# Linear attention with values and context as the stationary operands, two heads on two column halves of TensorE

## The chip, the core and the metric

The kernel runs on one core of a Trainium2 chip. The metric is the device time of one execution in microseconds (us), the median of several runs.

## The reference

On 1024 nodes of 512 features, a normalised `x` goes through a two-layer graph convolution and, beside it, through two Performer layers (linear attention with kernel features, then a feed-forward network); both results are added to `x`, and a mixture of experts follows. The kernel computes the Performer layers first. The change touches their attention alone. For each of the two layers, with 8 heads of 64 features and 256 random features (`M`), it is:

```python
qp = ratio * (exp(dd_q - diag_q - max_over_features) + 1e-4)     # (heads, nodes, 256)
kp = ratio * (exp(dd_k - diag_k - max_over_all) + 1e-4)          # (heads, nodes, 256)
k_sum = kp.sum(nodes)
d_inv = 1.0 / einsum('nm,m->n', qp, k_sum)
ctx   = einsum('nm,nd->md', kp, v)                               # (heads, 256, 64)
attn  = einsum('nm,md,n->nd', qp, ctx, d_inv)
x = x + (attn @ Wo + bo)
```

where `dd` are the projections of the queries and keys on the random features.

## The kernel before

All products run on TensorE; a large f32 product is written as three f32r products of high and low parts (L528 to L530), while the attention's own products are plain f32. PSUM is two rings of four banks of 128 x 512: ring A (`psA`), emptied mostly by ScalarE, and ring V (`psV`), emptied by VectorE. The order of use of every ring is written out by hand: `A_JOBS` and `MIX_V` number the jobs, TensorE waits until the job four places earlier has been emptied, and each emptying engine counts the jobs it has taken. The four engines' programs follow the same generator, `attention_order` (L127), so that the order of the work is one list.

The heads go in four pairs. A step `g` (16 in a layer, four to a pair) handles two node tiles of 128 for both heads of a pair. In a step:

- `ddq`: scores of the queries against the projection (`scores`, L627), one head on the upper and one on the lower 64 rows of the array, into two banks of ring A. VectorE takes the maximum over features (L1626) and forms the bias (L1629); ScalarE exponentiates into `work[:, 0:2]` (L1063).
- `ddk`: the same for the keys of the next pair, four tile pairs, two in each of a pair's first two steps; VectorE copies them out with a running maximum (L1532). GpSimd then takes the maximum over partitions (`kall`, L1317), VectorE forms `kbias` (`k_bias`, L1541), and ScalarE exponentiates the keys in place (`exp_k`, L1020).
- `tr`: eight transposes of the previous step's query exponentials (L712), so that features lie on partitions. ScalarE copies them back (`take_turned`, L1044), adding the constant 1e-4; `work[:, 2:4]` has one buffer, so this waits for the attention product before.
- `at`: the attention product of step g - 2 (L734 to L740): for each head, two node tiles and two halves of the features, the turned queries (128 x 128) stand in the array and 65 columns of the context move past: 64 values and the key sum. VectorE takes the reciprocal of the sum's column, 128 x 2 (L1634), and multiplies into `V` (L1636).
- `ctx`: in each pair's third step (L717 to L729): for each head and each half of the features, the key exponentials (128 x 128) stand and 130 columns of `V` move past: both heads' values, with a column of ones on each side, which gives the key sums. The constant 1e-4 enters as one more matmul with `vsum`, the values summed over tiles. VectorE copies the head's own 65 columns out (L1621).

After the last step the outputs, which have nodes on partitions, are turned by 32 transposes (L743 to L746, jobs `("o", h, k)` of ring A); ScalarE copies the high parts (L1078) and VectorE subtracts the low parts (L1646) into `hT`, and the output projection `wo` reads them (L748).

The queues: SP loads the weights, GpSimd splits them and reduces the key maxima in one queue of its own. In it a weight's split (`load(3, ...)`, waiting for the last query projection) lies between the key maxima of pairs 0 and 1.

## Time and profile before

| what | us |
|---|---|
| median of 3 runs (lowest, highest) | 1158.26 (1157.27, 1162.53) |
| the profiled execution's own time | 1157.11 |
| its span in the trace | 1155.3 |
| mean granted TensorE clock | 0.981 |

The profile is of one execution. A row of a group has the instruction's line in the kernel, engine, operation, the tiles written and read, shapes, count, busy time and mean duration. In the timeline a row merges instructions of the same kind that follow each other: its first start, the time from that to the end of its last, and their count. Matmuls overlap, so what one costs is the distance from its start to the next one's.

### The profile page before, as it was taken

The numbers are of one execution on the slowest core, as the hardware profiler recorded it, in microseconds if no ns is written. First come the engines' busy times: TensorE is split into PE (matmuls) and PEld (weight loads), VectorE is DVE, ScalarE is ACT, GpSimd is POOL, SyncE is SP. The second block draws the span as 40 slices with busy tenths as digits, with TensorE's granted clock in tenths as the row PEclk, the third lists the DMA queues.
The fourth block names the chain that finished last, engine by engine and source line by source line (L and its number), as shares of the span: only waits on it lengthen the run. The fifth ranks groups of instructions, "written<-read, shape, count | busy, mean of one in ns | idle before, by whom it ended". The sixth has DMA issues, their size and how long they took to land.

```text
span 1155.3 us, 16126 instructions
## 1 busy us (share of the span) xinstructions
PE 1083.4 (94%) x5992; PEld 881.8 (76%) x5992; DVE 707.9 (61%) x1530; ACT 366.2 (32%) x671; POOL 149.1 (13%) x141
## 2 busy tenths in 40 slices
PE   3999799999999999999898999999999999999986
PEld 2777699888777777776898977777778888777653
DVE  7576777479676567457665479764653117723667
ACT  4234466525321211136566325221300011001132
POOL 4230202000000000300202000000000705000036
PEclk8999999999999999999999999999999999999897
DMA  6230101002312112000101004211337201100001
GB/s 210 84 117 1 38 2 38 1 5 92 90 48 64 56 47 78 1 1 1 38 1 38 1 5 130 72 46 55 108 148 246 74 1 37 35 1 1 1 18 55
DMA packets 34654, 60.16 MB, mean 52 GB/s; under 512 B 19440, under 2 KB 20400, under 8 KB 33936
## 3 DMA queue, kind: packets, MB, share of 16 engines
q1 hardware_dynamic: 12688, 41.21, 10.9%
q10 hardware_dynamic: 21888, 17.87, 4.8%
q8 instruction: 53, 0.87, 0.3%
q14 instruction: 25, 0.20, 0.1%
HBM read 48.59 MB, written 10.49 MB: 51 GB/s over the span
## 4 chain that ended last, share of the span: by engine, by line
PE 79%; DVE 11%; ACT 4%; issue 4%; POOL 1%; DMA 0%; ACTq 0%; POOLq 0%; DVEq 0%
PE ps_a L528 10%; PE ps_a L530 10%; PE ps_a L529 10%; PE ps_v L528 10%; PE ps_v L529 9%; PE ps_v L530 9%; PE ps_a L885 5%; PE ps_v L725 4%; PE ps_v L736 3%; PE ps_a L549 2%; PE ps_a L660 2%; DVE expk L1532 2%; ACT work L1063 1%; DVE qmax L1626 1%; PE ps_v L614 1%
## 5 line engine op out<-in xcount | busy, mean ns | idle before, releaser
L528 PE MATMUL ps_a<-ht_hi,w_hi 128*128 128x512 f32 x488 | 193.8, 397 | 2.7 <-DVE w_lo L1798 0.9
L530 PE MATMUL ps_a<-ht_hi,w_lo 128*128 128x512 f32 x488 | 191.6, 393 | 0.0
L529 PE MATMUL ps_a<-ht_lo,w_hi 128*128 128x512 f32 x488 | 191.3, 392 | 0.0
L974 ACT ACTIVATE work<-ps_a,col_sb 128x512 f32<-128x512 f32 x96 | 66.7, 719 | 203.0 <-PE ps_a L530 144.7
L528 PEld LDWEIGHTS ps_a<-ht_hi,w_hi 128*128 128x128 f32 x488 | 92.5, 189 | 26.0 <-DVE headmask_r L1497 1.3
L1651 DVE TENSOR_TENSOR xm<-ps_v,xm 128x512 f32<-128x512 f32 x80 | 55.2, 690 | 86.0 <-PE ps_v L530 85.5
L530 PEld LDWEIGHTS ps_a<-ht_hi,w_lo 128*128 128x128 f32 x488 | 92.3, 189 | 19.9
L529 PEld LDWEIGHTS ps_a<-ht_lo,w_hi 128*128 128x128 f32 x488 | 92.4, 189 | 19.4
L528 PE MATMUL ps_v<-w_hi,f_hi 128*128 128x512 f32 x256 | 101.7, 397 | 0.0
L528 PE MATMUL ps_v<-w_hi,ht_hi 128*128 128x512 f32 x224 | 92.0, 411 | 9.7 <-issue 5.8
L530 PE MATMUL ps_v<-w_hi,f_lo 128*128 128x512 f32 x256 | 99.7, 389 | 0.0
L529 PE MATMUL ps_v<-w_lo,f_hi 128*128 128x512 f32 x256 | 99.6, 389 | 0.0
L529 PE MATMUL ps_v<-w_lo,ht_hi 128*128 128x512 f32 x224 | 89.8, 401 | 0.0
L530 PE MATMUL ps_v<-w_hi,ht_lo 128*128 128x512 f32 x224 | 89.5, 399 | 0.0
L1422 DVE CAST ht_hi<-work 128x512 fp32r<-128x512 f32 x56 | 33.1, 590 | 78.6 <-PE ps_a L530 65.2
L1063 ACT ACTIVATE work<-ps_a,qbias 128x256 f32<-128x256 f32 x128 | 50.5, 476 | 86.6 <-PE ps_a L549 71.1
L974 ACT ACTIVATE work<-ps_a,gcol_sb 128x512 f32<-128x512 f32 x24 | 16.5, 689 | 176.8 <-PE ps_a L530 171.8
L725 PE MATMUL ps_v<-v_sb,expk 128*128 128x130 f32 x512 | 63.2, 277 | 0.0
L736 PE MATMUL ps_v<-ctx_sb,work 128*128 128x65 f32 x512 | 61.8, 274 | 1.1 <-DVE ctx_sb L1621 0.6
L736 PEld LDWEIGHTS ps_v<-ctx_sb,work 128*128 128x128 f32 x512 | 59.6, 192 | 3.3 <-DVE expk L1532 1.6
L725 PEld LDWEIGHTS ps_v<-v_sb,expk 128*128 128x128 f32 x512 | 59.7, 191 | 1.1
L528 PEld LDWEIGHTS ps_v<-w_hi,ht_hi 128*128 128x128 f32 x224 | 43.5, 194 | 22.0 <-issue 9.5
(238 smaller groups left out, 1964.9 us busy)
## 6 DMA issues: line engine op xcount, KB each, us to landing
stage<-wstream SPq DMA_DIRECT2D x62, 512.0 KB, 3.7
adj_d<-adj_win ACTq DMA_DIRECT2D x16, 256.0 KB, 2.9
adj<-adj_d ACTq DMA_DIRECT2D x2, 2048.0 KB, 12.3
xt_d<-xt_hi SPq DMA_DIRECT2D x2, 1024.0 KB, 5.0
xt_d<-xt_lo SPq DMA_DIRECT2D x1, 2048.0 KB, 11.4
ht_hi<-xt_d ACTq DMA_DIRECT2D x1, 2048.0 KB, 7.7
ht_lo<-xt_d ACTq DMA_DIRECT2D x1, 2048.0 KB, 12.4
x_again<-x ACTq DMA_DIRECT2D x8, 256.0 KB, 9.3
```

What stands on the lines that cost most here:

```text
L528: nc.tensor.matmul(ps, left[0], right[0], start=first, stop=False)
L529: nc.tensor.matmul(ps, left[0], right[1], start=False, stop=False)
L530: return nc.tensor.matmul(ps, left[1], right[0], start=False, stop=last)
L549: last = nc.tensor.transpose(ps[:, nodes(n)], source, ident[:])
L660: nc.tensor.matmul(ps, hot_low[:, c, :], hot_key[:, c, :], start=c == 0, stop=False)
L725: nc.tensor.matmul(context, expk[g % 2][:, j, t, nodes(m)], V[:, t, g, :], start=t == 0, stop=False)
L736: last = nc.tensor.matmul(ps[:, n * (DH + 1):(n + 1) * (DH + 1)], work[:, 2 + j, nodes(2 * m + n)], ctx_sb[:, pair % 2, j, m, :], start=m ...
L885: nc.tensor.matmul(ps, Pr[i][:, t, nodes(m)], adj[:, t, half(h)].bitcast(f32r), start=False, stop=False)
L974: nc.scalar.activation(work[:, n % 4, :], psA[:, i % BANKS, :], func, **how).then_inc(a_empty, 1)
L1063: last = nc.scalar.activation(work[:, j, M * n:M * (n + 1)], psA[:, i % BANKS, M * n:M * (n + 1)], ACT.Exp, scale=DN, bias=qbias[:, g % 4, ...
L1422: nc.vector.tensor_copy(hi, work[:, n % 4, :]).then_inc(high, 1)
L1651: nc.vector.tensor_tensor(Xm[:, t, :], ps, Xm[:, t, :], ALU.add).then_inc(v_empty, 1)
```

## The change

What it does, in the order of the diff:

- The order of the steps is new. The context of a pair is made in two halves of four node tiles: the first at the end of the fourth step of the pair before (for pair 0 at the end of step 0), the second at the end of the pair's second step. Key scores of the next pairs come in a pair's first and third step, those of the third step behind the turns.
- `context`: the values of one head (128 x 64) stand in one column half of the array, those of the other head in the other, and 256 columns of key exponentials move past each. The constant 1e-4 is one full-width matmul ahead of the first half. Key sums come from ones standing in 32 columns: two heads by two tiles on four column quarters.
- VectorE copies the first half into `ctx_t` and adds the second. `turn_context` transposes the two value blocks, and two matmuls against a head mask gather the sums; VectorE copies these to `ctx_sb`, scaling the sums.
- `attend`: the context of each head (128 x 64), and then its key sum repeated over 64 columns, stand in a column half; 256 columns of turned queries move past. Outputs come out with features on partitions, and the sums already repeated over them. One bank holds both heads.
- VectorE's reciprocal is over 128 x 256, its product over 128 x 256.
- The 32 output transposes and their eight jobs are gone. ScalarE copies the high parts from `V` to `hT`, three blocks in each of steps 14 and 15 and two at the end; VectorE subtracts the low parts, three behind each of the attention steps 12 and 13 and two at the end. The output projection waits for 7 of 8 parts for its first four tiles and for all for the others.
- ScalarE exponentiates the keys tile by tile, four activations in each step. `k_bias` of the next pair moves from VectorE's third step to its second.

The diff, cut to its core (on TensorE, then ScalarE, then VectorE):

```diff
 def attention_order():
         if g < STEPS:
             yield "ddq", g
-            if s < 2 and pair + 1 < NH // 2:
-                yield "ddk", g
-        if s == 2 and g < STEPS:
-            yield "ctx", pair
+            if s == 0 and pair + 1 < NH // 2:
+                yield "ddk", (pair + 1, range(0 if g == 0 else 2, 4))
+            if s == 2:
+                yield "turn_ctx", pair
         if 1 <= g <= STEPS:
             yield "tr", g - 1
+        if s == 2 and pair + 2 < NH // 2:
+            yield "ddk", (pair + 2, range(2))
         if g >= 2:
             yield "at", g - 2
+        if g == 0 or s == 3 and pair + 1 < NH // 2:
+            yield "ctx", (0 if g == 0 else pair + 1, 0)
+        if s == 1 and g < STEPS:
+            yield "ctx", (pair, 1)
+
+OUT_PARTS = [(pair, h) for h in range(H) for pair in range(NH // 2 - 1)] + [(NH // 2 - 1, h) for h in range(H)]
...
+                ones = V[:, 0, 0, 0:1]
+
+                def context(pair, part_):
+                    ps = bank("v", ("ctx", pair, part_))
+                    tiles = range(NT // 2 * part_, NT // 2 * (part_ + 1))
+                    pe.wait_ge(expk_done, L * NH * NT + 2 * NT * pair + NT * (part_ + 1))
...
+                    if part_ == 0:
+                        nc.tensor.matmul(ps[:, 0:M], vsum[:, pair, 1:1 + P], eps_k[:].to_broadcast([P, M]), start=True,
+                                         stop=False)
+                    for t in tiles:
+                        for j in range(2):
+                            nc.tensor.matmul(ps[DH * j:DH * (j + 1), 0:M], V[:, t, pair, 1 + DH * j:1 + DH * (j + 1)],
+                                             expk[pair % 2][:, j, t, :], start=part_ == 1 and t == tiles[0],
+                                             stop=t == tiles[-1])
+                    for t in tiles[0::2]:
+                        for j in range(2):
+                            for i in range(2):
+                                n = 2 * j + i
+                                last = nc.tensor.matmul(ps[32 * n:32 * (n + 1), M:2 * M], ones.to_broadcast([P, 32]),
+                                                        expk[pair % 2][:, j, t + i, :], start=t == tiles[0],
+                                                        stop=t == tiles[-2])
...
+                def turn_context(pair):
+                    ps = bank("v", ("turn_ctx", pair))
+                    written_v(("ctx", pair, 1))
+                    for m in range(MT):
+                        nc.tensor.transpose(ps[:, nodes(m)], ctx_t[:, nodes(m)], ident[:])
+                    for m in range(MT):
+                        last = nc.tensor.matmul(ps[:, M + 2 * m:M + 2 * (m + 1)], ctx_t[:, nodes(MT + m)], headmask[:, 0, 0:2],
+                                                start=True, stop=True)
...
+                def attend(g):
+                    pair, s = divmod(g, NT // 2)
+                    ps = bank("v", ("at", g))
+                    if s == 0:
+                        written_v(("turn_ctx", pair))
+                    written_a(("tr", g, 1))
+                    for columns, values in ((slice(0, M), slice(0, DH)), (slice(M, 2 * M), slice(DH, DH + 1))):
+                        for m in range(MT):
+                            for j in range(2):
+                                left = ctx_sb[:, pair % 2, m, j, values]
+                                last = nc.tensor.matmul(ps[DH * j:DH * (j + 1), columns],
+                                                        left.to_broadcast([P, DH]) if columns.start else left,
+                                                        work[:, 2 + j, M * m:M * (m + 1)], start=m == 0, stop=m == MT - 1)
+                                if columns.start and m == MT - 1:
+                                    last.then_inc(at_half if j == 0 else v_full, 1)
...
-                written_v(("at", STEPS - 1, 1))
-                for h in range(H):
-                    for k in range(KT):
-                        turn(bank("a", ("o", h, k)), [V[:, 4 * h + n, k, 1:1 + P] for n in range(4)], a_full)
                 slot = weight_slot("o")
                 for t in range(NT):
-                    written_a(("o", t // 4, KT - 1))
+                    pe.wait_ge(o_split, L * H * KT + (len(OUT_PARTS) if t >= 4 else len(OUT_PARTS) - 1))
...
                         if g:
-                            act.wait_ge(v_full, v0 + (MIX_V[("at", g - 1, j)] + 1))
+                            act.wait_ge(*((v_full, v0 + (MIX_V[("at", g - 1)] + 1)) if j else (at_half, L * STEPS + g)))
...
+                def high_out(pair, h):
+                    act.wait_ge(v_empty, v0 + done(MIX_V[("at", 4 * pair + 2 * h + 1)]))
+                    nc.scalar.activation(hT[0][:, pair, half(h)].rearrange("p (t n) -> p t n", n=P), V[:, 4 * h:4 * h + 4, pair, 1:1 + P],
+                                         ACT.Copy).then_inc(o_high, 1)
...
+                    pair = (g + 3) // 4
+                    if 0 < pair < NH // 2:
+                        part_ = (s + 3) % 4
+                        exp_k(pair, 4 * part_, 4 * (part_ + 1))
+                    if g == STEPS - 2:
+                        act.wait_ge(v_full, v0 + (MIX_V[("ctx", NH // 2 - 1, 1)] + 1))
+                    if g >= STEPS - 2:
+                        for n in range(3 * (g - STEPS + 2), 3 * (g - STEPS + 3)):
+                            high_out(*OUT_PARTS[n])
                 take_turned(STEPS - 1)
...
+                def take_attended(g):
+                    pair, s = divmod(g, NT // 2)
+                    ps = job("at", g)
+                    dve.wait_ge(at_half, L * STEPS + g + 1)
+                    nc.vector.reciprocal(rden[:, g % 2, :], ps[:, M:2 * M]).then_inc(rden_done, 1)
+                    dve.wait_ge(rden_done, L * STEPS + g + 1)
+                    nc.vector.tensor_tensor(V[:, 2 * s:2 * s + 2, pair, 1:1 + P], ps[:, 0:M].rearrange("p (t n) -> p t n", n=P),
+                                            rden[:, g % 2, :].rearrange("p (t n) -> p t n", n=P), ALU.mult).then_inc(v_empty, 1)
...
+                    elif what == "ddq":
+                        bound_queries(g)
+                        if g % 4 == 1 and g // 4 + 1 < NH // 2:
+                            k_bias(g // 4 + 1)
+                    elif what == "ctx":
+                        pair, part_ = g
+                        if L == 0 and part_ == 1 and pair < 3:
+                            (blocks, keys, bounds)[pair]()
+                        take_context(pair, part_)
...
+                    elif what == "at":
+                        if g == STEPS - 1:
+                            low_out(len(OUT_PARTS) - 2)
+                        take_attended(g)
...
+                        if STEPS - 4 <= g < STEPS - 2:
+                            for n in range(3 * (g - STEPS + 4), 3 * (g - STEPS + 5)):
+                                low_out(n)
+                low_out(len(OUT_PARTS) - 1)
```

## Rows read from the trace of the kernel before

**Rows 1.** The page: busy time, share of the span and instructions of each engine.
```profile
PE 1083.4 (94%) x5992; PEld 881.8 (76%) x5992; DVE 707.9 (61%) x1530; ACT 366.2 (32%) x671; POOL 149.1 (13%) x141
```

**Rows 2.** Window: a pair of layer 0. Length; PE, PEld, DVE, ACT, POOL busy; clock; DMA.
```profile
171.73:199.00 27.27, 26.06 (x265) 24.85 (x265) 20.24 (x66) 17.59 (x41) 7.04 (x5) 1.00 0.10 26
```

**Rows 3.** Timeline of TensorE: start, time to the last one's end, instruction, count [idle before].
```profile
130.09 1.95 PE L725 MATMUL ps_v<-v_sb,expk 128*128 128x130 f32 x16
131.87 0.39 PE L727 MATMUL ps_v<-vsum,eps_k 128*128 128x130 f32 x2
...
137.72 1.97 PE L736 MATMUL ps_v<-ctx_sb,work 128*128 128x65 f32 x16 [0.57 <-DVE ctx_sb L1621]
...
218.09 1.90 PE L736 MATMUL ps_v<-ctx_sb,work 128*128 128x65 f32 x16
```

**Rows 4.** Timeline of TensorE: key scores on two row halves, then transposes.
```profile
121.74 0.28 PE L633 MATMUL ps_v<-proj_hi,k_part 64*128 64x256 f32 x2
121.86 0.28 PE L633 MATMUL ps_v<-proj_lo,k_part 64*128 64x256 f32 x2
...
123.04 0.28 PE L633 MATMUL ps_v<-proj_hi,k_part 64*128 64x256 f32 x2
123.25 1.09 PE L549 MATMUL ps_a<-ident,work 128*128 128x128 f32 x8
```

**Rows 5.** Timeline of TensorE: 8 stationary columns (L614) between products with 128.
```profile
100.53 0.39 PE L530 MATMUL ps_a<-ht_hi,w_lo 128*128 128x512 f32 x1
100.76 0.40 PE L614 MATMUL ps_v<-sq_hi,headmask_r 128*8 128x512 f32 x1
...
101.23 0.39 PE L528 MATMUL ps_a<-ht_hi,w_hi 128*128 128x512 f32 x1
```

**Rows 6.** Waits of TensorE: us in total, times, longest.
```profile
PE ps_a L633 <- ACT work L1063: 15.6, 12, 2.8
```

**Rows 7.** Timeline of GpSimd: the key maximum of pair 1, layers 0 and 1.
```profile
135.78 0.37 POOL L1317 PARTITION_ALL_REDUCE kall<-kmax  x1 [7.30 <-issue]
...
562.60 0.37 POOL L1317 PARTITION_ALL_REDUCE kall<-kmax  x1 [7.38 <-issue]
```

**Rows 8.** Groups by line: instructions, busy us, mean ns | idle before, releasers.
```profile
L1063 ACT ACTIVATE work<-ps_a,qbias 128x256 f32<-128x256 f32 x128 | 50.5, 476 | 86.6 <-PE ps_a L549 71.1 <-DVE qbias L1629 14.7
L1626 DVE TENSOR_REDUCE qmax<-ps_a 128x2 f32<-128x512 f32 x64 | 43.7, 684 | 13.3 <-PE ps_a L633 13.3
L1051 ACT ACTIVATE work<-ps_a,eps_k 128x512 f32<-128x512 f32 x64 | 42.9, 701 | 5.1 <-PE ps_v L736 4.7
...
L1636 DVE TENSOR_TENSOR v_sb<-ps_v,rden 128x128 f32<-128x128 f32 x64 | 18.7, 292 | 2.2
...
L1642 DVE TENSOR_TENSOR xm<-xm,rows_sb 128x512 f32<-128x512 f32 x16 | 12.3, 767 | 0.0
...
L1634 DVE RECIPROCAL rden<-ps_v 128x2 f32<-128x2 f32 x64 | 10.7, 167 | 24.5 <-PE ps_v L736 24.2
...
L1078 ACT ACTIVATE ht_hi<-ps_a 128x512 fp32r<-128x512 f32 x16 | 8.9, 600 | 6.2 <-PE ps_a L549 6.2
```

**Rows 9.** Timeline of TensorE at both layers' ends of attention; a window of layer 1.
```profile
228.86 4.52 PE L549 MATMUL ps_a<-ident,v_sb 128*128 128x128 f32 x32 [0.59 <-DVE v_sb L1636]
233.14 0.48 PE L528 MATMUL ps_v<-w_hi,ht_hi 128*128 128x512 f32 x1
...
644.24 1.90 PE L736 MATMUL ps_v<-ctx_sb,work 128*128 128x65 f32 x16
...
655.01 5.67 PE L549 MATMUL ps_a<-ident,v_sb 128*128 128x128 f32 x32 [0.59 <-DVE v_sb L1636]
660.44 0.48 PE L528 MATMUL ps_v<-w_hi,ht_hi 128*128 128x512 f32 x1
...
655.00:657.00 2.00, 1.99 (x10) 1.99 (x11) 0.28 (x1) 0.65 (x2) 0.00 (x0) 0.53 0.00 0
```

**Rows 10.** One line's instructions (L1869): duration ns min/median/max, starts, form.
```profile
L1869 DVE RECIPROCAL gate<-gate x2: 177/178/178, 1071.7 to 1114.4; 128x4 f32<-128x4 f32 x2
```

More of the change, by code:

```diff
@@ L118 @@
     + query_ring()
-    + [("o", h, k) for h in range(H) for k in range(KT)]
     + ffn_ring_a()
@@ L155, in ring_v_attention @@
         if what == "ddk":
-            yield from ddk_jobs(*ddk_ahead(g))
-            if g == 0:
+            yield from ddk_jobs(*g)
+            if g[0] == 1:
                 yield "turned", 3
-        elif what in ("ctx", "at"):
-            yield from ((what, g, j) for j in range(2))
+        elif what == "ctx":
+            yield (what, *g)
+        elif what in ("turn_ctx", "at"):
+            yield what, g
 MIX_V = numbered(
@@ L698, in mix_layer @@
                 sum_squares(len(QK_ORDER) - 1)
+                ones = V[:, 0, 0, 0:1]
[3 more added lines that the diff above has]
+                    pe.wait_ge(expk_done, L * NH * NT + 2 * NT * pair + NT * (part_ + 1))
+                    if pair == 0 and part_ == 0:
+                        pe.wait_ge(vsum_added, L * (NT - 1) + NT)
+                    if part_ == 0:
[13 more added lines that the diff above has]
+                                                        stop=t == tiles[-2])
+                                if t == tiles[-2]:
+                                    last.then_inc(*((v_full, 1) if n == 3 else (ctx_parts, 1)))
@@ L743, in mix_layer @@
[L743 to L746 removed]
+                    elif what == "ctx":
+                        context(*g)
+                    elif what == "turn_ctx":
+                        turn_context(g)
+                    else:
+                        attend(g)
                 slot = weight_slot("o")
@@ new lines, in bound_queries @@
+                def bound_queries(g):
+                    pair, s = divmod(g, NT // 2)
+                    for j in range(2):
+                        i = MIX_A[("ddq", g, j)]
+                        dve.wait_ge(a_full, a0 + (i + 1))
+                        nc.vector.tensor_reduce(qmax[:, g % 2, j, :], psA[:, i % BANKS, :].rearrange("p (t m) -> p t m", m=M),
+                                                axis=AX.X, op=ALU.max).then_inc(qmax_done, 1)
+                        dve.wait_ge(qmax_done, L * 2 * STEPS + (2 * g + j + 1))
+                        nc.vector.scalar_tensor_tensor(out=qbias[:, g % 4, j, :], in0=qmax[:, g % 2, j, :], scalar=-DN,
+                                                       in1=ndiag[:, 0, 2 * s:2 * s + 2, 2 * pair + j], op0=ALU.mult,
+                                                       op1=ALU.add).then_inc(qbias_ready, 1)
@@ L1607, in mix_layer @@
                 for what, g in attention_order():
-                    pair, s = divmod(g, NT // 2)
                     if what == "ddk":
-                        ddk(*ddk_ahead(g))
-                        if g == 0:
+                        ddk(*g)
+                        if g[0] == 1:
                             take_turned(3)
-                        continue
-                    if what == "tr":
-                        continue
-                    if what == "ctx" and L == 0 and g < 3:
-                        (blocks, keys, bounds)[g]()
```

109 lines of the change are left out of this document (36 added, 73 removed).

## The prediction

> **What bounds the kernel now.** I read the page's busy shares first: TensorE is busy 94% of the span, VectorE 61%, ScalarE 32% [rows 1], so time is lost or won on TensorE. Then a stage by windows: one pair of heads in the middle of layer 0's attention takes 27.27 us, with TensorE busy 26.06, VectorE 20.24 and ScalarE 17.59 [rows 2]; each layer has four. So a pair costs what TensorE does in it plus about 1.2 us of waits, and the change must be priced in TensorE's instructions.
>
> Next, the pitch of these instructions (the distance of starts; durations overlap). Every plain f32 matmul is two records, each with its own weight load. In the context product 16 records of 130 columns start within 1.78 us, 0.111 each; in the attention product 16 records of only 65 columns take (1.90 - 0.27) / 15 = 0.108 each [rows 3]. Half the columns at the same pitch: the 65-column records wait for their 128-column weight loads, and at 130 columns the streaming just shows above that. So before: a pair's context is 72 records, 4 x 18 x 0.111 = 8.0 us, and a step's attention 16 x 0.108 = 1.74 us, 6.96 a pair.
>
> **What the records cost after.** Stationary and moving operands change places: 256 columns now move past 64 or 32 stationary ones. No row shows a 256-column f32 record. Below, it cannot beat the f32r scores, whose 256 columns pass once in about 0.12 [rows 4]; above, streaming that grows with the columns gives 0.111 x 256 / 130 = 0.22. I take T = 0.22, because the 130-column record is the nearest row and lies above the weight-load pitch.
>
> Do two column halves run at once? No row shows it; two row halves do: the scores come as pairs (x2), one pair per 0.12 us [rows 4]. I take it that column halves can too; if not, each record costs a full T. But a score is one record, and an f32 matmul is two. Issued in program order, the second record of head 0 waits for the first (same columns), and the first record of head 1 stands behind it. So records overlap in steps: head 0's second with head 1's first, and so on; n matmuls take (n + 1) T. With four quarters nothing more is won in this order: again one matmul per T, not four per 2 T.
>
> **The sum, part by part, for a pair.** Attention: 8 matmuls a step, 9 T = 1.98 us, 7.92 a pair (before 6.96). Context, first half: eps matmul 2 T, eight value matmuls, eight ones matmuls, one T to run out, 19 T; second half 17 T; together 36 T = 7.92 (before 8.0). Turning the context: two transposes and two matmuls against the head mask, 6 records at 0.11 = 0.66. Together 16.5 against 14.96: **+1.54 a pair, +6.2 a layer**. Three of the 16 attention steps lie in the tail, counted apart below: 0.7 of the 6.2 goes there, 5.5 stays.
>
> Changing between tile shapes: from half rows to full rows the scores' last pair starts at 123.04, frees the array at 123.16, and the transposes start at 123.25: 0.09 [rows 4]. From 128 to 8 stationary columns and back, 3 starts in 0.70 us, 0.23 each [rows 5], is the pitch of matmuls that change nothing, so I count column shapes at nothing (at most 0.09 each, some eight a pair, 6 us in all). Key scores moved behind the turns add a trip or two: +0.3 a layer.
>
> Waits in the steps. TensorE waits 15.6 us in all for ScalarE's exponentials, in 12 waits up to 2.8 [rows 6]; two of about 2.8 lie at the layers' starts, which leaves 5.0 a layer. With half a context behind every second step there is always cover for them: they go. In their place comes a smaller one: the attention product is now signalled for both heads almost together, so ScalarE starts to empty the next turned block (2 x 0.70 [rows 8]) only at its end. TensorE has the query scores (6 x 0.12 + 0.09 = 0.8 [rows 4]) and half of the eight turns (4 x 0.11 = 0.45) to do, then waits about 0.35 for the second bank, in the steps with no context before them, 8 a layer: 2.8. Net -2.2 a layer.
>
> Start of a layer. GpSimd's key maximum of pair 1 comes at 135.78 after 7.30 us of its own delay, and likewise in layer 1 [rows 7]; nothing here moves it. VectorE now waits for it one step earlier, ahead of taking the second context half, so the bias scalars and the block numbers of layer 0 (three or four short operations of about 0.17 each, like the reciprocal of 2 columns [rows 8], 0.7 for either) and the add (0.7) put the context's turn at about 138.2. Before, TensorE began its first attention product at 137.72 [rows 3] with one block of turns (0.9) more behind it: **+1.4 a layer**; the bounds are 0 (later steps absorb it) and 2.8. The pause of some 4 us ahead of it can cost clock as well: at the end of layer 1's attention, behind a pause of only 0.59 us, the granted clock stood at 0.53, near the lower level of 1.2 GHz, and 32 turns took 5.67 us, where layer 0's took 4.52 [rows 9].
>
> Tail. Before, from the end of step 12's attention (218.09 + 1.74 = 219.8; layer 1: 644.24 + 1.74 = 646.0) to the output projection at 233.14 and 660.44 [rows 3, 9]: 13.3 and 14.5 us, with 32 output turns, their copies and subtractions inside. All that goes; the copies out (0.60 each [rows 8]) move into steps 14 and 15 and the subtractions onto VectorE between steps. After, from the same point: ScalarE empties step 13's turned block 1.6, three copies 1.8, the last subtraction 0.7, like the maximum over as many columns [rows 8] (4.1), and only then VectorE, whose order has them ahead, bounds step 15 for the first head 0.85 (4.95); four exponentials 1.9 (6.85); emptying step 14's block 1.4 (8.25); the turns' second half 0.45 (8.7); attention 14, 1.98 (10.7); emptying block 15, 1.6 (12.3); attention 15, 1.98: 14.3. The output projection follows, since its first four tiles need only 7 of 8 parts and cover the last (10.9 us). So +1.0 in layer 0, -0.2 in layer 1: the saved turns are given back in a chain through ScalarE and VectorE.
>
> VectorE: of 20.24 a pair go 8 x (0.167 + 0.292) [rows 8] and two context copies of about 0.29; new are the context's copy, add and split (2.0) and per step a reciprocal of 256 columns and a product of 256 (0.42, from 0.292 for 128). The reciprocal is not in the trace at that width: 2 columns take 0.167, 4 take 0.178 [rows 8, 10], 5.5 ns a column more, so 1.6 for 256; the end below is 0.42, as the product. With 1.6 VectorE has 26.1 a pair, under TensorE's 28: hidden. The Trainium skill ("VectorE: DVE Perf Modes", the fixed hardware budget) says that a reciprocal divides iteratively with a repeat count of 8; at that page's 0.96 GHz my estimate is 2.3 us. By it VectorE would come to 28.9 a pair, about TensorE's, and the sum would be some 8 us higher. The rows' slope lies between one cycle and eight; no wide row decides.
>
> Sum: layer 0 5.5 + 0.3 - 2.2 + 1.4 + 1.0 = 6.0, layer 1 4.8, together +11 on the profiled execution's 1157.1: 1168. That execution lies 1.2 under the median of the runs, 1158.3, so **1169**.
>
> **The rivals.** (1) *Each column tile keeps its own queue*, so tiles overlap whatever the program order: attention 8 T, context 2 T + 16 T + 8 T (four quarters at once): 7.04 + 5.72 + 0.66 = 13.4 a pair, 3.1 under the forecast, 24.8 in all: **1144**. For it: the row pairs start together at no loss [rows 4]. Against it: single records cannot show what a second one does. It decides the sign: of a pair's 72 T the change may keep about 65, and once a matmul costs under 0.9 T it wins. The Trainium skill ("TensorE: Matmul & The Clock Gate", Part 3) says that matmuls keep program order in start and end and only weight loads are pulled ahead, which is the forecast's case.
> (2) *A 256-column record streams once*, T = 0.117: attention 4.2, context 4.2, 9.1 a pair. TensorE falls under VectorE, which then bounds a pair at 26.1 in the first half of a layer and less in the second, where four additions to the residual of 0.77 [rows 8] are over (23.0): 2.7 a pair under before, 21 in all, less 3 for start and tail: **1140**. Against it: 130 columns above 65 in pitch [rows 3].
> (3) *Halves do not overlap at all*, the change not doing what it says: 16 T and 66 T, 14.1 + 14.5 + 0.66 = 29.3 a pair, 12.8 over the forecast: **1271**. For it: no row has f32 on column tiles.
>
> **How the numbers follow.** A measurement can tell some 0.5% here, 5.8 us: faster is under 1152.5, slower over 1164. Forecast 0.43, its own range 1158 to 1182 (column switches, reciprocal, clock, start): 0.13 same, 0.30 slower. Rival 1, 0.33, from 1132 to 1156: 0.30 faster, 0.03 same. Rival 2, 0.10, faster. Rival 3, 0.14, slower. So 0.40 faster, 0.16 same, 0.44 slower. The range 1132 to 1184 leaves out rival 3 and part of rival 2.
>
> **What would show it.** After: the value and ones matmuls at one per 0.22 in each group (0.11 per ones matmul: rival 1; 0.44 per matmul: rival 3); 9 T from the first record of an attention step to the next group; a wait of some 4 us ahead of the context's turn at each layer's start; a reciprocal near 1.6 us; about 14 us from step 12's attention to the output projection; no output turns. The forecast is wrong if a middle pair takes under 27 us or over 30.

## The result, and the profile after

The changed kernel takes 1168.76 us (median of four runs, 1166.44 to 1171.35) against 1157.76 for the kernel before in the same comparison: ratio 1.0092, 95% interval 1.0051 to 1.0133. The forecast was 1169. The total was met; the profile shows that two large errors in it cancelled.

The busy line of the page, which answers to [rows 1]:

```profile
PE 1085.5 (93%) x5912; PEld 825.6 (71%) x5928; DVE 756.1 (65%) x1482; ACT 367.2 (31%) x671; POOL 148.5 (13%) x141
```

TensorE's busy time is nearly the same; VectorE has 48 us more. To see where the time went I cut the span at two marks, each layer's first query score and the first matmul of its output projection. These are the two attention stages, by windows (from:to, length; PE, PEld, DVE, ACT, POOL busy; granted clock; DMA share, GB/s), first of the kernel before:

```profile
114.71:233.14 118.43, 106.69 (x1047) 100.40 (x1047) 76.88 (x235) 69.79 (x157) 15.46 (x12) 1.00 0.06 19
541.51:660.44 118.93, 107.81 (x1047) 102.08 (x1047) 72.36 (x214) 69.73 (x157) 14.32 (x11) 0.99 0.06 19
```

and of the kernel after, with one pair in the middle of layer 1 (this answers to [rows 2]), and two short stretches:

```profile
114.27:245.44 131.17, 112.45 (x1015) 76.25 (x1015) 100.79 (x211) 70.62 (x157) 15.43 (x12) 0.90 0.05 17
550.50:669.14 118.64, 105.89 (x1015) 70.97 (x1014) 94.68 (x190) 70.52 (x157) 14.27 (x11) 0.96 0.06 19
599.15:625.67 26.52, 25.60 (x264) 17.56 (x265) 24.41 (x53) 17.60 (x40) 1.34 (x2) 1.00 0.00 1
124.91:128.52 3.61, 3.61 (x17) 1.72 (x17) 0.00 (x0) 0.00 (x0) 3.30 (x2) 0.50 0.41 145
168.16:171.98 3.82, 3.82 (x23) 3.49 (x24) 1.33 (x5) 1.68 (x4) 0.00 (x0) 0.50 0.00 0
```

Layer 0 lost 12.7 us, layer 1 gained 0.3. Both layers run the same change, so it is not the price of the new matmuls that made the loss. A pair in layer 1 takes 26.52 us where it took 27.27 [rows 2].

TensorE's timeline in that pair (start, time to the last one's end, instruction, count [idle before]) answers to [rows 3]:

```profile
599.15 0.41 PE L737 MATMUL ps_v<-ident,ctx_t 128*128 128x128 f32 x2 [0.81 <-DVE ctx_t L1674]
...
599.76 1.07 PE L556 MATMUL ps_a<-ident,work 128*128 128x128 f32 x8
...
606.53 1.95 PE L753 MATMUL ps_v<-work,ctx_sb 128*64 128x256 f32 x16
608.40 0.70 PE L716 MATMUL ps_v<-eps_k,vsum 128*128 128x256 f32 x2
609.03 1.95 PE L720 MATMUL ps_v<-expk,v_sb 128*64 128x256 f32 x16
610.91 1.07 PE L727 MATMUL ps_v<-expk,v_sb 128*32 128x256 f32 x16
611.91 0.39 PE L640 MATMUL ps_a<-proj_hi,q_part 64*128 64x256 f32 x2
...
619.28 1.95 PE L753 MATMUL ps_v<-work,ctx_sb 128*64 128x256 f32 x16
621.06 1.90 PE L720 MATMUL ps_v<-expk,v_sb 128*64 128x256 f32 x16
622.88 1.07 PE L727 MATMUL ps_v<-expk,v_sb 128*32 128x256 f32 x16
623.88 0.39 PE L640 MATMUL ps_a<-proj_hi,q_part 64*128 64x256 f32 x2
```

From start to start: eight matmuls on two column halves take 1.88 us (609.03 to 610.91; 1.78 where another group on halves follows, 619.28 to 621.06), eight on four quarters only 1.00 (610.91 to 611.91). The quarters' single records start four at a time, within 0.02 us, at 610.91, 611.15, 611.37 and 611.59. A pair's attention is 3 x 1.88 + 1.78 = 7.4, its context 3.51 + 2.82 = 6.3, the turn 0.61: 14.4 us, where the forecast had 16.5 and the kernel before 14.96.

In layer 0, TensorE's timeline has these rows:

```profile
120.49 0.38 PE L640 MATMUL ps_v<-proj_hi,k_part 64*128 64x256 f32 x2 [1.84 <-DVE expk L1572]
...
124.91 3.68 PE L720 MATMUL ps_v<-expk,v_sb 128*64 128x256 f32 x16
...
167.71 0.66 PE L737 MATMUL ps_v<-ident,ctx_t 128*128 128x128 f32 x2 [3.37 <-DVE ctx_t L1674]
168.16 0.85 PE L739 MATMUL ps_v<-headmask,ctx_t 128*128 128x2 f32 x4
168.87 1.95 PE L556 MATMUL ps_a<-ident,work 128*128 128x128 f32 x8
...
201.00 0.66 PE L737 MATMUL ps_v<-ident,ctx_t 128*128 128x128 f32 x2 [5.30 <-DVE ctx_t L1674]
```

Two waits at the turn of the context, 3.37 and 5.30 us, stand where layer 1 has 0.81, and behind the first the same eight transposes take 1.95 us instead of 1.07: the granted clock there is 0.50, the lower level of 1.2 GHz (window 168.16:171.98 above). At the start of either layer it falls too, behind a wait of 1.84 for VectorE to empty the key scores: the eight value matmuls at 124.91 take 3.68 at clock 0.50. From turn to turn, pair 1 ends 30.4 us after pair 0 in layer 0 and pair 2 another 33.3 after it; in layer 1 both take 26.5.

What VectorE does ahead of the turn at 201.00, by its own timeline:

```profile
192.96 1.75 DVE L1686 RECIPROCAL rden<-ps_v 128x256 f32<-128x256 f32 x1
194.74 0.42 DVE L1688 TENSOR_TENSOR v_sb<-ps_v,rden 128x256 f32<-128x256 f32 x1
195.08 0.68 DVE L1712 TENSOR_TENSOR xm<-xm,rows_sb 128x512 f32<-128x512 f32 x1
195.68 0.63 DVE L1634 SCALAR_TENSOR_TENSOR reached<-block_all,window_no,group_no 128x136 f32<-128x136 f32 x2
...
197.19 1.84 DVE L1642 TENSOR_TENSOR bound<-bound,span 128x1 f32<-128x1 f32 x1
...
200.16 0.69 DVE L1674 TENSOR_TENSOR ctx_t<-ps_v,ctx_t 128x512 f32<-128x512 f32 x1
```

No row has idle time before it: VectorE is simply late. From 195.68 to 200.16 it computes the window bounds of the graph part, which only layer 0 does, and only then adds the second context half for which TensorE waits. Before, the same jobs stood ahead of the context copies too, but under 8 us of context matmuls, and took 2.15 us (186.53 to 188.68). Here they take 4.48, because two instructions on one column each last 1.84 and 0.77 us (197.19 and 199.26) where they lasted 0.16. The first row is of the kernel before, the second of the changed one:

```profile
188.03 0.16 DVE L1602 TENSOR_TENSOR bound<-bound,span 128x1 f32<-128x1 f32 x1
...
196.68 2.33 POOL L1295 TENSOR_TENSOR w_lo<-stage,w_hi 128x1024 fp32r<-128x1024 f32 x1 [7.05 <-issue]
```

Each of the two ends 0.01 to 0.02 us after an instruction of GpSimd's weight split. It is so in all four runs in which they fall on that split (the changed kernel, r_after, e3 and e7: 1.48 to 1.92 and 0.76 to 0.77); in the others they last 0.16 each. So 2.3 us of the wait of 5.30 go with this meeting of VectorE and GpSimd; no run moved the split alone.

The waits of TensorE (us in total, times, longest), which answer to [rows 6]: the 15.6 us that the scores waited for ScalarE's exponentials are gone, 4.2 for them remain in the two tails (1.9 and 0.17 in either, ahead of step 14's transposes), and the context's sum has come in their place.

```profile
PE ps_v L737 <- DVE ctx_t L1674: 13.3, 6, 5.3
...
PE ps_a L556 <- ACT work L1101: 4.2, 4, 1.9
PE ps_v L640 <- DVE expk L1572: 4.2, 4, 1.8
```

### The profile page after: what moved, and what is told of

Its sections match the earlier page's. It is cut to its first block, busy times and chain, and to the rows that moved or that the text cites. A ratio compares the mean times of both kernels' runs of the same rounds, so it can differ in the third digit from the quotient of the medians.

```text
span 1167.3 us, 15958 instructions
## 1 busy us (share of the span) xinstructions
PE 1085.5 (93%) x5912; PEld 825.6 (71%) x5928; DVE 756.1 (65%) x1482; ACT 367.2 (31%) x671; POOL 148.5 (13%) x141
## 4 chain that ended last, share of the span: by engine, by line
PE 78%; DVE 13%; issue 5%; POOL 2%; ACT 1%; DMA 0%; POOLq 0%; ACTq 0%; DVEq 0%
PE ps_a L535 10%; PE ps_a L536 10%; PE ps_a L537 10%; PE ps_v L535 9%; PE ps_v L537 9%; PE ps_v L536 9%; PE ps_a L918 5%; PE ps_v L753 4%; PE ps_a L556 3%; PE ps_a L667 2%; DVE rden L1686 2%; DVE qmax L1660 1%; PE ps_a L640 1%; PE ps_v L720 1%; DVE expk L1572 1%
## 5 line engine op out<-in xcount | busy, mean ns | idle before, releaser
L535 PEld LDWEIGHTS ps_a<-ht_hi,w_hi 128*128 128x128 f32 x488 | 92.0, 188 | 25.8 <-DVE headmask_r L1537 1.3
L537 PEld LDWEIGHTS ps_a<-ht_hi,w_lo 128*128 128x128 f32 x488 | 92.0, 189 | 19.8
L753 PE MATMUL ps_v<-work,ctx_sb 128*64 128x256 f32 x512 | 66.4, 404 | 7.5 <-ACT work L1084 3.2
L1007 ACT ACTIVATE work<-ps_a,gcol_sb 128x512 f32<-128x512 f32 x24 | 16.5, 689 | 176.9 <-PE ps_a L537 172.2
L1686 DVE RECIPROCAL rden<-ps_v 128x256 f32<-128x256 f32 x32 | 56.2, 1756 | 19.6 <-PE ps_v L753 19.3
L535 PEld LDWEIGHTS ps_v<-w_hi,ht_hi 128*128 128x128 f32 x224 | 43.1, 192 | 22.6 <-issue 10.3
L753 PEld LDWEIGHTS ps_v<-work,ctx_sb 128*64 128x64 f32 x512 | 37.2, 144 | 28.3 <-issue 9.1
```

Of the source, the lines that this page charges most:

```text
L535: nc.tensor.matmul(ps, left[0], right[0], start=first, stop=False)
L537: return nc.tensor.matmul(ps, left[1], right[0], start=False, stop=last)
L753: last = nc.tensor.matmul(ps[DH * j:DH * (j + 1), columns], left.to_broadcast([P, DH]) if columns.start else left, work[:, 2 + j, M * m:M ...
L1007: nc.scalar.activation(work[:, n % 4, :], psA[:, i % BANKS, :], func, **how).then_inc(a_empty, 1)
L1686: nc.vector.reciprocal(rden[:, g % 2, :], ps[:, M:2 * M]).then_inc(rden_done, 1)
```

## The experiments

**The theory** after this comparison: TensorE got cheaper, and the loss comes from VectorE's order, which TensorE now waits for (the preparations in layer 0, the start, the tail), and from the clock that falls behind these waits. **Rivals**: VectorE is hidden and the loss lies in TensorE's own instructions; or VectorE is simply too full with its wide reciprocal.

All results, from each kernel's own profile and runs. "All else" is the span without the two attention stages. No edit touches it, and yet it goes from 912.5 to 922.2, so the theories are judged by the stages, and the runs by their intervals. A stage's time is that of one execution: the two of the changed kernel differ by 0.9 us in layer 0 and 0.5 in layer 1. Where it matters, times are also counted from the stage's first score, which in layer 0 comes between 111.99 and 114.86.

```
                layer 0  layer 1  both    all else  median us (before's)   ratio, 95% interval
before          118.43   118.93   237.36  917.94
after           131.17   118.64   249.81  917.49    1168.76 (1157.76)  1.0092  1.0051 to 1.0133
r_after         132.05   118.11   250.16  919.94    1166.83 (1161.34)  1.0061  1.0030 to 1.0093
e1_prep         121.70   120.85   242.55  920.35    1162.04 (1159.87)  1.0016  0.9986 to 1.0046
e2_copy         122.87   116.97   239.84  922.16    1162.25 (1159.87)  1.0005  0.9972 to 1.0039
e3_order        132.62   124.76   257.38  921.22    1178.62 (1159.87)  1.0153  1.0108 to 1.0197
e4_prepadd      121.82   117.71   239.53  919.77    1163.10 (1159.87)  1.0036  1.0010 to 1.0063
e5_tailbias     119.16   120.07   239.23  914.77    1156.69 (1161.34)  0.9969  0.9937 to 1.0002
e6_start        120.79   119.51   240.30  912.50    1163.75 (1161.34)  1.0028  0.9994 to 1.0062
e7_startonly    131.36   121.95   253.31  919.99    1174.66 (1161.34)  1.0125  1.0070 to 1.0180
e8_latebias     115.82   114.16   229.98  921.82    1152.97 (1158.06)  0.9937  0.9911 to 0.9964
```

**The changed kernel again (r_after).** No edit.

> The changed kernel once more, unchanged, so that it has times on the chip of the other runs of this call. If the loss is steady: 1.005 to 1.013 of the kernel before, with the two long waits at layer 0's context turns (3 to 5 us) there again. If those waits were chance: below 1.004.

Measured 1.0061, with the waits at layer 0's turns there again: 3.37 and 5.38. The loss is steady, and by the stages all of it lies in layer 0. Layer 0's start went another way in this execution:

```profile
124.16 1.95 PE L720 MATMUL ps_v<-expk,v_sb 128*64 128x256 f32 x16
...
137.43 0.66 PE L737 MATMUL ps_v<-ident,ctx_t 128*128 128x128 f32 x2 [4.62 <-DVE ctx_t L1674]
```

Behind the same wait of 1.84 the clock did not fall (1.95 us where it was 3.68), and the time came back as a longer pause ahead of the first turn, 4.62 instead of 1.96.

**The preparations out of the way (e1_prep).**

```diff
-                        if L == 0 and part_ == 1 and pair < 3:
-                            (blocks, keys, bounds)[pair]()
+                        if L == 0 and part_ == 1 and pair == 0:
+                            blocks()
...
                         take_turned_context(g)
+                        if L == 0 and g == 2:
+                            bounds()
...
                         take_attended(g)
+                        if L == 0 and g == 9:
+                            keys()
```

> Two of layer 0's three graph preparations are moved on VectorE, nothing is left out: the edge keys go behind taking step 9's attention, the window bounds behind taking pair 2's turned context, where VectorE waits for TensorE anyway. Theory (VectorE's queue): in layer 0 they stand ahead of the addition of the second context half, and TensorE waits for it at the context's turn (3.37 us for pair 1, 5.30 us for pair 2); then its clock falls. So both waits drop to about 1 us or less, as in layer 1 (0.81), layer 0's attention goes from 131.2 to about 121 us, layer 1's stays at 118.6, the run at about 1158. Rival (the loss is TensorE's own instructions, or the tail's order, or the burst of key scores at the start): layer 0 stays over 128, the run over 1165.

TensorE's timeline at layer 0's four turns:

```profile
137.49 0.41 PE L737 MATMUL ps_v<-ident,ctx_t 128*128 128x128 f32 x2 [1.91 <-DVE ctx_t L1674]
164.00 0.41 PE L737 MATMUL ps_v<-ident,ctx_t 128*128 128x128 f32 x2 [0.84 <-DVE ctx_t L1674]
190.53 0.41 PE L737 MATMUL ps_v<-ident,ctx_t 128*128 128x128 f32 x2 [0.81 <-DVE ctx_t L1674]
217.57 0.41 PE L737 MATMUL ps_v<-ident,ctx_t 128*128 128x128 f32 x2
```

Both long waits are down to what layer 1 has, pairs 1 and 2 now take 26.5 us each, and layer 0's stage went from 131.2 to 121.7: shown. VectorE's busy time in the stage did not fall (101.06 against 100.79). It was the place of some 7 us of work, not its amount. The run missed its 1158 by 4 us. The kernel before was 2.1 us slower in this comparison than in the first (1159.87 against 1157.76), and layer 1 lost 2.2: in its tail, behind a pause of 1.93, the clock was 0.55 and one attention group took 3.43 us instead of 1.95.

**The reciprocal taken out (e2_copy).**

```diff
-                    nc.vector.reciprocal(rden[:, g % 2, :], ps[:, M:2 * M]).then_inc(rden_done, 1)
+                    nc.vector.tensor_copy(rden[:, g % 2, :], ps[:, M:2 * M]).then_inc(rden_done, 1)
```

> The reciprocal of the 256 denominators is replaced by a copy of the same 256 columns (so the outputs are multiplied by the denominators: the division is left out); everything else stays. VectorE should lose 1.756 - 0.42 = 1.3 us in each of 16 steps a layer. Theory (VectorE's queue bounds the first half of a layer): the wait at pair 1's and pair 2's context turn in layer 0 falls by about two steps' worth, 2.7 us each, the starts of the two layers lose about a microsecond, layer 0's attention goes from 131.2 to about 123, layer 1's from 118.6 to about 115: the run at 1155 to 1158. Rival (VectorE is hidden behind TensorE, as the forecast had it): within 3 us of 1168.

VectorE's busy time fell by 20.1 us in layer 0's stage (100.79 to 80.66). The two waits went from 3.37 to 1.27 and from 5.30 to 0.89, and layer 0's stage from 131.2 to 122.9, as expected; layer 1 gained 1.7 of the 3.6 expected. So the late addition has two causes in one queue, the preparations and the reciprocals ahead of them, and either one taken away is nearly enough. The second wait fell by 4.4 where 2.7 was expected: the bounds now run ahead of GpSimd's split, and their two instructions take 0.16 each again. The run, 1162.25, stayed over the expected 1155 to 1158; all else took 922.2 in its profile.

**The order of the column tiles (e3_order).** One half's four value matmuls (or a quarter's two ones matmuls, or a half's two attention matmuls) come one after another, then the next tile's.

```diff
-                    for t in tiles:
-                        for j in range(2):
+                    for j in range(2):
+                        for t in tiles:
                             nc.tensor.matmul(ps[DH * j:DH * (j + 1), 0:M], ...
```

> Only the program order of the matmuls on column halves and quarters changes: all of one half's (or quarter's) matmuls of a group come before the next one's, instead of taking turns. Nothing is left out. If records overlap only with their neighbours in program order (the forecast's steps), 8 value matmuls on two halves take about 15 T = 3.2 us instead of 1.9, 8 attention matmuls about 12 T = 2.6 instead of 1.9, the 8 ones matmuls about 12 T = 2.6 instead of 1.0: 6 to 7 us a pair, the run near 1215. If each column tile had a queue of its own that holds several matmuls, the groups keep 1.9, 1.9 and 1.0 us and the run stays near 1168.

TensorE's timeline in a pair of layer 1:

```profile
610.14 2.00 PE L753 MATMUL ps_v<-work,ctx_sb 128*64 128x256 f32 x16
612.06 0.39 PE L640 MATMUL ps_a<-proj_hi,q_part 64*128 64x256 f32 x2
...
616.70 2.86 PE L720 MATMUL ps_v<-expk,v_sb 128*64 128x256 f32 x16
619.49 1.09 PE L727 MATMUL ps_v<-expk,v_sb 128*32 128x256 f32 x16
620.51 0.39 PE L640 MATMUL ps_a<-proj_hi,q_part 64*128 64x256 f32 x2
```

Runs of two matmuls per tile cost nothing: attention 1.92 against 1.88, quarters 1.02 against 1.00. Runs of four cost 0.9: 2.79 against 1.88, short of the 3.2 of strict steps and of the 3.5 of no overlap (16 x 0.22). So tiles do overlap across program order, but not without a limit. A tile that holds one record at work and three waiting would give both numbers: four records of two matmuls fit, so the next tile starts at once; of eight, the other half's first can start when the fifth begins, 4 T late, 12 T = 2.6 in all. The single records agree: four start alone, some 0.22 apart, from 616.70 to 617.40, and from 617.62 on they start in two rows, each 0.22 apart. What holds the other half back is not measured by itself. Both expectations were wrong in part.

**The residual's additions later (e4_prepadd).** The moves of e1, and:

```diff
-                        if g < NT:
-                            nc.vector.tensor_tensor(Xm[:, g, :], Xm[:, g, :], rows_sb[:, 2, :], ALU.add)
+                        if 4 <= g < NT + 4:
+                            nc.vector.tensor_tensor(Xm[:, g - 4, :], Xm[:, g - 4, :], rows_sb[:, 2, :], ALU.add)
```

> The moves of the run before, and the eight additions of a row to the residual (0.68 us each on VectorE) go from steps 0 to 7 to steps 4 to 11, out of the stretch in which VectorE also empties the most key scores. Nothing is left out. Theory (VectorE's queue bounds the first half of a layer): layer 0's attention near 119 us, layer 1's near 117.5, the run 1154 to 1157, 1 to 3 under the run with the moves alone. Rival (VectorE does not bound there once the preparations are gone): equal to the run with the moves alone within 1 us.

Layer 0's stage stayed where it was (121.82 against 121.70), as the rival had it; layer 1 is 3.1 shorter, of which the tail's clock is the larger part (17.1 us from the last turn to the projection, against 18.7). But the rival's reason does not hold. From the first turn to the second, where the additions are gone, a pair takes 25.80 us in both layers against 26.51 and 26.52 in e1, and the wait of 0.8 at that turn is gone; with the reciprocal out (e2) layer 1's pairs take 25.80 too. So VectorE's amount of work still costs some 0.7 us in such a pair. In layer 0 the additions then stand with e1's moved edge keys, and the last pair takes 29.66 against 27.04, a lower clock included (0.88 against 0.94).

**The two ends (e5_tailbias).** Besides e1's moves:

```diff
-                        if g % 4 == 1 and g // 4 + 1 < NH // 2:
+                        if g % 4 == 1 and 1 < g // 4 + 1 < NH // 2:
                             k_bias(g // 4 + 1)
...
-                            blocks()
+                            after_context.append(blocks)
                         take_context(pair, part_)
+                        if part_ == 1 and pair == 0:
+                            k_bias(1)
+                            for job_ in after_context:
+                                job_()
...
-                        if STEPS - 4 <= g < STEPS - 2:
-                            for n in range(3 * (g - STEPS + 4), 3 * (g - STEPS + 5)):
+                        if g == STEPS - 3:
+                            for n in range(6):
                                 low_out(n)
```

> Besides the moved preparations, two more places of VectorE's queue, nothing left out. At a layer's start pair 1's bias (which waits for GpSimd's maximum until 135.5) and the block numbers go behind the addition of pair 0's second context half; at the tail the first three low parts of the output (1.9 us) go behind the bounds of step 15 and step 13's attention. Theory (what is left over the kernel before is VectorE's order at the two ends of a layer): the first context turn comes at 135.3 instead of 137.5, -2 us a layer; the tail loses 1.9 us of chain, and 1.5 more where the pause of 1.9 no longer lets the clock fall, -2 to -3.4 a layer; the run 8 to 11 us under the one with moved preparations, 1151 to 1154. Rival (TensorE's matmuls are what is left, or other waits end last right behind): within 3 us of 1162.

At the tail the pause ahead of step 14's transposes (1.93 us in e1) went, and the clock stayed up: from the last turn to the projection 16.8 us in both layers, against 18.6 and 18.7. That is 1.8 and 1.9 less, under the 2 to 3.4 expected, because the projection itself now waits: 1.02 us in layer 0 and 1.31 in layer 1, where it starts 0.1 us behind the seventh low part, which the program has it wait for.

```profile
659.49 0.68 DVE L1650 TENSOR_TENSOR ht_lo<-v_sb,ht_hi 128x512 fp32r<-128x512 f32 x1
660.27 0.47 PE L535 MATMUL ps_v<-w_hi,ht_hi 128*128 128x512 f32 x1 [1.31 <-issue]
```

Where the clock had stayed up without the move, the same stretch took 17.2 (the changed kernel's layer 1), so the order alone gave some 0.4 us and the clock the rest. The start did not do what was expected. The first turn came at 135.5, as forecast, but the first attention product only 0.9 us sooner than in e1 in layer 0 (139.97 against 140.87, 0.7 from the first score), and in layer 1 0.2 later (26.0 us from the first score against 25.8). TensorE's waits say why:

```profile
PE ps_v L640 <- DVE ctx_sb L1679: 4.7, 2, 3.8
```

They are 0.97 us in layer 0 and 3.78 in layer 1. VectorE stands at the bias, waiting for GpSimd's maximum, and behind it in the queue is the taking of the turned context (L1679), whose bank TensorE needs for pair 2's key scores. The wait moved by one place. The two stages together fell by 3.3 us, not 8 to 11.

**The start's order alone (e7_startonly).**

```diff
-                yield "ddk", (pair + 1, range(0 if g == 0 else 2, 4))
+                yield "ddk", (pair + 1, range(0, 2) if g == 0 else range(2, 4))
...
             yield "ctx", (0 if g == 0 else pair + 1, 0)
+            if g == 0:
+                yield "ddk", (1, range(2, 4))
```

> Only the start's order is changed against the changed kernel (key scores of pair 1 in two halves with the first half of pair 0's context between them); the preparations, the bias and the tail stay. Nothing is left out. Theory: TensorE's pause and the slow clock there go, but VectorE then has the key maximum half a microsecond later, GpSimd's maximum comes at about 136, and the first context turn, which stands behind the bias on VectorE, stays at 137.5 to 138.5: nothing gained, 1167 to 1170. Rival (the slow clock at the start is what costs): the first turn moves ahead by 3 us or more, the run at 1162 or less.

```profile
120.93 1.95 PE L722 MATMUL ps_v<-expk,v_sb 128*64 128x256 f32 x16
...
137.90 0.66 PE L739 MATMUL ps_v<-ident,ctx_t 128*128 128x128 f32 x2 [6.00 <-DVE ctx_t L1676]
...
139.07 1.95 PE L558 MATMUL ps_a<-ident,work 128*128 128x128 f32 x8
```

The slow clock at the start is gone (1.95 where it was 3.68), and the turn comes at 137.90 all the same: the time became a pause of 6.00 us. Nothing gained, as expected; and behind the longer pause the clock fell, so the eight transposes took 1.95 instead of 1.07, which the expectation had not counted. The run came out at 1175 instead of 1167 to 1170, where the changed kernel took 1167 in the same comparison.

**All of it (e6_start)**: e5's moves and e7's together.

> The same, and the first half of pair 0's context stands between the two halves of pair 1's key scores, so that TensorE has work while VectorE empties the first four banks. Nothing is left out. Theory (the burst of eight key-score blocks makes TensorE wait 1.84 us, and the fall of the clock behind it doubles the next 3.5 us of context): the wait at 118.9 goes, the context's first half takes 3.5 instead of 6.3 us, another 3 to 4 us a layer less than the run before, 1144 to 1148, as long as the first context turn isn't held by something else. Rival (the bias for pair 1 or the exponentials hold the start): the same as the run before within 2 us.

The rival held: 240.30 for both stages against 239.23. TensorE is ahead sooner (turn at 129.49), and then waits 4.25 us (4.5 in layer 1) at the same place behind the same bias; the first attention product comes at 137.90, 25.6 us from the first score, as in e5. The median of the runs is 7.1 us over e5's in the same comparison, which the stages do not show; the two intervals overlap.

**The bias further back (e8_latebias).** On e6:

```diff
                         if g[0] == 1 and 3 in g[1]:
                             take_turned(3)
+                        if g[0] == 2 and 0 in g[1]:
+                            k_bias(1)
...
                         if part_ == 1 and pair == 0:
-                            k_bias(1)
...
-                        exp_k(pair, 4 * part_, 4 * (part_ + 1))
+                        if g != 1:
+                            exp_k(pair, 0 if g == 2 else 4 * part_, 4 * (part_ + 1))
```

> All moves together (preparations, start's order, tail), and pair 1's bias goes further back: on VectorE behind emptying the first key scores of pair 2, and on ScalarE the first exponentials of pair 1 go from step 1 to step 2, so that nothing in the first two steps waits for GpSimd's maximum (135.5 to 136). Nothing is left out. Theory (the start is held by VectorE's and ScalarE's order behind that maximum, no longer by TensorE): the first attention product comes at 133 to 135 instead of 137.9, 3 to 4 us a layer, the profiled span at about 1146 against 1152.8, and the runs 0.985 to 0.993 of the kernel before. Rival (the maximum or the clock takes the time back in the next step): within 2 us of the run with the start's order, ratio 0.995 to 1.003.

```profile
129.39 0.41 PE L739 MATMUL ps_v<-ident,ctx_t 128*128 128x128 f32 x2
...
132.96 1.95 PE L755 MATMUL ps_v<-work,ctx_sb 128*64 128x256 f32 x16
```

The first attention product comes at 132.96, 20.8 us from the first score and 4.8 sooner than in e6, and the stages take 115.82 and 114.16 us: 10.3 less than e6, 19.8 less than the changed kernel, 7.4 less than before. That is more than the 3 to 4 us a layer expected. The ratio of the runs is 0.9937 (0.9911 to 0.9964), just outside the expected 0.985 to 0.993, but under both kernels': 0.9937 x 1158.06 is 7.3 us under before, with 4.2 to 10.3 in the interval, about what the stages gained. The profiled span, 1151.8, stayed over the 1146 expected because all else took 921.8 in this execution.

## Why the prediction was right in its total and wrong in its parts

By the forecast's own sign, a middle pair between 27 and 30 us, it was wrong: such pairs took 26.5 in layer 1 and 30.4 and 33.3 in layer 0. Two of its steps failed, in opposite directions.

**TensorE's price: the step that failed most.** The forecast's strict program order ("with four quarters nothing more is won in this order") made a pair 1.54 us dearer. T = 0.22 was right: 1.78 us for eight matmuls on halves is 8 T. But matmuls of several tiles run at once even when program order puts two or four records of one tile ahead: quarters took 1.00 instead of 8 T = 1.76, twice a pair, and every group ended without the extra T. So a pair came out 0.6 us cheaper than before. This is rival 1's mechanism, with 14.4 us a pair where it had 13.4; the rest is the eps matmul (0.63 where two T are 0.44), the quarters (1.00 where four T are 0.88) and up to 0.1 us more where halves are followed by another tile shape (1.82 to 1.88 against 1.78), so a change of tile shape is not free, though I counted it at nothing. The error is 2.1 us in each of eight pairs, some 17 us. The Trainium skill ("TensorE: Matmul & The Clock Gate", Part 3) has matmuls keep program order in start and end. The traces do not agree for f32 matmuls of two records on column tiles: in strict order the quarters could not fall under 1.76, and they took 1.00 by turns and 1.02 in e3's runs of two.

**VectorE "hidden": the step that failed on the other side.** The reciprocal was well sized: 1.6 forecast, 1.756 measured.

```profile
L1686 DVE RECIPROCAL rden<-ps_v 128x256 f32<-128x256 f32 x32 | 56.2, 1756 | 19.6 <-PE ps_v L753 19.3
```

The estimate of 2.3 worked out from the Trainium skill ("VectorE: DVE Perf Modes", the fixed hardware budget) was too high. A middle pair has VectorE busy 24.41 of 26.52 us (forecast 26.1 of 28), and on average that is nearly hidden: e2 and e4 make it 0.7 us a pair. But the sum compared shares and not the queue: VectorE works in order, the graph preparations of layer 0 stand ahead of the context's sum, and after the change TensorE has nothing to do until that sum. I had seen the block numbers at pair 0 (0.7) and missed the keys and bounds at pairs 1 and 2. They cost 3.9 and 6.8 us over layer 1's pairs, clock included (30.4 and 33.3 against 26.5), 2.3 of the second with GpSimd's split. e1 shows it.

**The other steps.** The waits for ScalarE's exponentials inside the steps went, as forecast. The start was forecast +1.4 a layer; from the first score to the first attention product it is 27.5 against 23.0 before in layer 0 and 25.5 against 22.4 in layer 1: +4.5 and +3.1. Of this 1.8 is no loss: two tiles of key scores, 1.76 us at 600.76 to 602.52 in the pair above, now come ahead of that product. It leaves 2.7 and 1.4. The pause ahead of the turn was shorter than forecast (2.0 and 1.0, not 4), because the clock had already fallen behind the burst of key scores and TensorE came late; that burst was not in my sum. Where the clock did not fall there, in r_after, the pause was 4.62. The tail was forecast at 14.3 us and took 14.9 (from 228.69 + 1.88) and 13.2; the three subtractions ahead of step 15's bounds are in it as forecast, and in e5 moving them gave 1.8 to 1.9 us a layer, of which 0.4 without the clock.

Per layer the sum was +6.0 and +4.8; measured +12.7 and -0.3. Layer 1 shows mainly the error on TensorE, layer 0 the two together. The forecast case met the total by luck. Rival 1 had the better price for TensorE and missed the total (1144), because it too took VectorE's queue for hidden; with that queue put in order, e8 gains 7.3 us, about half of what rival 1 promised.

## What to carry to other kernels

When a change takes cover off a hand-over between two engines, list what stands ahead of the hand-over in the other engine's queue, layer by layer and step by step; a busy share under that of the bound engine says nothing about it. A wait that goes often moves one place down the same queue (e5 at both ends, e6), and time won ahead of a fixed late arrival, here GpSimd's maximum, is only a longer pause that costs clock as well (e7): move the consumers of the late value back until nothing near the bound engine stands behind them (e8). And judge small edits by the stretch that they touch, where the rest of the program varies by more than the edit is worth.

## What was not expected of the hardware

Eight f32 matmuls of 256 columns on four column quarters take 1.00 us, on two halves 1.78 to 1.88; one matmul on all 128 columns (two records) takes 0.63 up to the next group. The overlap survives two matmuls in a row on one tile, and loses 0.9 us with four. One-column instructions of VectorE with two tensors as inputs (TENSOR_TENSOR) took 0.76 to 1.92 us instead of 0.16 where they fell on GpSimd's weight split; the one-input instruction between them (L1643, 199.07) took its usual 0.15.

The length of a pause of TensorE did not decide by itself whether its clock fell. The pause of 1.84 at a layer's start was followed by granted clock 0.50 to 0.52 in both layers of the changed kernel, and by 1.00 in layer 0 of e2 and of r_after. That of 1.96 before the changed kernel's first turn was followed by 2.85 us at 0.50 (138.90 to 141.75), that of 1.91 in e1 by none. Behind 3.37 (the changed kernel's second turn) and 6.00 (e7's first) the clock stood at 0.50 to 0.51; behind the pauses of 0.81 in layer 1 it stayed at 1.00. What else decides was not tried.
